# Layer-0 attention by half-groups, with the scores turned on TensorE

## What is computed

```python
# layer 0: 16 heads of 8 features
tp = silu(cond) @ Wt + bt                       # shift, scale and gate, twice, per sequence
h = layernorm(x, g1, be1) * (1 + scale_msa) + shift_msa
q, k, v = split(h @ Wqkv + bqkv)                # [B, 32, 16, 8] each
attn = softmax(einsum('blhd,bmhd->bhlm', q, k) * 8 ** -0.5)
h = einsum('bhlm,bmhd->blhd', attn, v) @ Wproj + bproj
x = x + gate_msa * h
h = layernorm(x, g2, be2) * (1 + scale_mlp) + shift_mlp
x = x + gate_mlp * (gelu(h @ W1 + b1) @ W2 + b2)
# layer 1: rmsnorm, FiLM, one head of 128 features, the same MLP without gates
```

## Time and profile before

| | |
|---|---|
| median of three runs | 284.4 us |
| profiled execution | 283.33 us, span 281.5 us |
| PE busy | 248.0 us (88% of the span) |
| DVE, ACT, POOL busy | 189.0, 164.7, 184.7 us |
| PE's clock, granted | 0.994 of full on average |
| chain that ended last | PE 55%, DVE 11%, DMA 10%, ACT 8%, issue 8% |
| DMA packets | 44569, of which 32512 under 512 B |

### The profile page before, as it was taken

One profiled execution on the slowest core, in us unless ns is written; L12 is line 12 of the kernel. 1 busy time (PEld: TensorE's weight loads), 2 busy tenths in 40 slices (PEclk: granted clock), 3 DMA queues, 4 the chain that ended last, 5 costly groups with the idle time before them and its releaser, 6 DMA issues.

```text
span 281.5 us, 8249 instructions
## 1 busy us (share of the span) xinstructions
PE 248.0 (88%) x2876; PEld 186.7 (66%) x2876; DVE 189.0 (67%) x535; ACT 164.7 (59%) x358; POOL 184.7 (66%) x187
## 2 busy tenths in 40 slices
PE   0677848689889898888999999999999989999996
...
GB/s 226 316 201 44 151 125 183 91 79 63 63 77 92 74 83 110 215 63 2 1 0 0 0 0 0 2 2 1 2 0 0 0 5 37 37 37 37 40 37 75
DMA packets 44569, 18.11 MB, mean 64 GB/s; under 512 B 32512, under 2 KB 43136, under 8 KB 44032
## 3 DMA queue, kind: packets, MB, share of 16 engines
...
q10 hardware_dynamic: 576, 1.98, 2.0%
...
## 4 chain that ended last, share of the span: by engine, by line
PE 55%; DVE 11%; DMA 10%; ACT 8%; issue 8%; SPq 3%; POOL 3%; ACTq 1%; DVEq 1%; POOLq 0%
PE bank L1086 20%; PE bank L948 17%; PE bank L978 5%; DMA values_scratch<-Vs 5%; PE bank L923 3%; DMA Vx<-values_scratch 3%; PE bank L991 2%; DVE hA L481 2%; ACT Kx L771 2%; DMA X<-x 2%; PE bank L1007 2%; ACT squares L886 2%; ACT xhat L756 2%; SPq L239 1%; PE bank L955 1%
## 5 line engine op out<-in xcount | busy, mean ns | idle before, releaser
L756 ACT ACTIVATE xhat<-X,shift,rstd 128x128 f32 (+1 forms) x96 | 39.4, 483 | 53.9 <-POOL shift L297 53.6
L1086 PE MATMUL bank<-W,Qx 128*128 128x128 f32 x512 | 59.6, 275 | 0.0
L1086 PEld LDWEIGHTS bank<-W,Qx 128*128 128x128 f32 x512 | 58.5, 192 | 1.0 <-issue 1.0
L948 PE MATMUL bank<-h,W 128*128 128x512 f32 x128 | 58.3, 595 | 0.0
L308 POOL TENSOR_TENSOR h<-hA,B 128x512 f32<-128x512 f32 x32 | 34.0, 1064 | 23.9 <-DVE hA L481 23.7
L806 ACT ACTIVATE Qx<-bank,col 128x512 f32<-128x512 f32 x64 | 39.1, 678 | 8.6 <-PE bank L948 8.6
L481 DVE TENSOR_TENSOR hA<-bank,A 128x512 f32<-128x512 f32 x32 | 22.0, 688 | 32.4 <-PE bank L923 16.6
L978 PE MATMUL bank<-Kx,Qx 128*128 128x128 f32 x256 | 35.4, 282 | 5.5 <-DMA Qx<-Qs 1.9
L948 PEld LDWEIGHTS bank<-h,W 128*128 128x128 f32 x128 | 22.9, 190 | 22.7 <-issue 22.4
L978 PEld LDWEIGHTS bank<-Kx,Qx 128*128 128x128 f32 x256 | 31.1, 192 | 7.4 <-DMA Qx<-Qs 2.1
L339 POOL TENSOR_TENSOR X<-yG,xg 128x512 f32 (+1 forms) x16 | 20.4, 1274 | 18.6 <-DVE yG L490 18.6
...
## 6 DMA issues: line engine op xcount, KB each, us to landing
values_scratch<-Vs SPq DMA_DIRECT2D x8, 288.0 KB, 2.4
...
Qx<-Qs SPq DMA_DIRECT2D x28, 64.0 KB, 2.3
...
```

What stands on the lines that cost most here:

```text
L756: last = act.activation(xhat[:, p, P * t:P * (t + 1)], X[:, x_tile(gg, t), :], ACT.Identity, bias=shift[:, p, t:t + 1], scale=rstd[:, p, t ...
L948: last = pe.matmul(bank[2 + n][:, :], w(f"W1_{phase // 2}", n), h[:, p, :], start=True, stop=True)
L1086: last = pe.matmul(y[t // 2][:, P * t:P * (t + 1)], gT[:, p, n, P * t:P * (t + 1)], w(f"W2_{phase // 2}", n), start=(n == 0), stop=(n == N ...
```

## The change

In layer-0 attention the unit becomes half a group: eight sequences, whose scores lie in two banks, the even sequences in bank 4 and the odd ones in bank 5.

- **Scores.** The keys, not the queries, are now spread over four masked copies, by four DMAs of 32 rows of 2 KB (`spread_k`); for groups 0 and 1 ACT and DVE make the copies (`place_k`). `Qx` is gone. Each sequence has four products of 32x32 weights with 128 columns, one for each quarter of PE's rows: 64 a group.
- **Turning.** The 32x32 transposes on DVE are replaced by 128x128 transposes on PE, eight for each half (`scores_T`), and the exponential reads them from PSUM.
- **Order.** PE's step is written anew and looped over groups 1 to 6; while it weighs the last quarter of a half it already waits for what the next scores need.
- **The last groups.** In group 6 the loop's queries and keys of "group 8" are the first two chunks of the MLP: their weights are loaded over Wq and Wk (`wup_in`), and ACT applies gelu to them there.
- **Values and gates.** The scratch buffer holds values by partition, so that a row is 2304 B in the store and 576 B in the loads. The first gate comes in eight pieces of a group each, one after each group's keys and values, the second in four pieces.
- **Update.** Bias, gate and residual are three passes: DVE adds the bias, POOL multiplies by the gate and POOL adds x. `keep` is gone from the first two phases.
- **Small ones.** -mean and var+eps in phase 0 are `tensor_reduce` instead of `tensor_scalar`. `bcol`, the memset of `Qx` and the masked query writes on DVE at the start are gone. The fold of the biases moves from the setup into group 0.

```diff
+        def of_half(half):
+            return range(half * GB // 2, (half + 1) * GB // 2)
+
+        def slot(b):
+            return b % (GB // 2) // 2
+
...
-            def spread_q(g, p):
-                wait(sp, s_ready, 4 * g - 4)
-                sp.wait_ge(qkv_moved, 2 * g + 1)
-                for a in range(HQ):
-                    sp.dma_start(Qx[L * a:L * (a + 1), p, :, a, :], by_seq(Qs[L * a:L * (a + 1), p, :])).then_inc(q_spread[p], 16)
...
+                sp.wait_ge(k_moved, g + 1)
+                sp.wait_ge(s_ready, 2 * g - 2)
+                for r in range(HQ):
+                    sp.dma_start(Kx[r:P:HQ, p, r, :], Ks[r:P:HQ, p, :]).then_inc(k_spread[p], 16)
+
+            def spread_v(g, p):
+
+                sp.wait_ge(v_moved, g + 1)
+                wait(sp, v_spread[p], 16 * HQ * (g // 2))
+                sp.dma_start(values_d[p], Vs[:, p, :]).then_inc(v_stored[p], 16)
+                sp.wait_ge(v_stored[p], 16 * (g // 2 + 1))
+                wait(sp, pv_done, 2 * g - 2)
+                src = values_d[p].rearrange("(q m) (r f) -> r m q f", q=TB, r=HQ)
+                for r in range(HQ):
+                    sp.dma_start(Vx[L * r:L * (r + 1), p, r, :].rearrange("m (q f) -> m q f", q=TB),
+                                 src[r]).then_inc(v_spread[p], 16)
+
+            def spread_gates(i, n, pieces):
+
+                size = NT // pieces
+                tiles = slice(n * size, (n + 1) * size)
+                wait(sp, gates_in[i], 16 * TB * n)
+                for b in range(TB):
+                    sp.dma_start(gate[L * b:L * (b + 1), i, tiles, :].rearrange("p t d -> p (t d)"),
+                                 gates_d[b:b + 1, i, tiles, :].rearrange("o t d -> o (t d)")
+                                 .broadcast_to([L, size * D])).then_inc(gates_in[i], 16)
...
+            spread_gates(0, 0, NG)
+            for g in range(1, NG):
+                spread_v(g, g % 2)
+                if g < NG - 1:
+                    spread_k(g + 1, (g + 1) % 2)
+                if g == NG - 2:
+                    sp.wait_ge(k_ready, NG)
+                    sp.wait_ge(q_ready, NG)
+                    at, up0 = W_AT["Wqkv"][0], W_AT["W1_0"][0]
+                    sp.dma_start(W[:, at:at + 2 * D], weights[:, up0:up0 + 2 * D]).then_inc(wup_in, 16)
+                spread_gates(0, g, NG)
+            sp.wait_ge(pv_done, 2 * NG - 1)
+            for n in range(NG // 2):
+                spread_gates(1, n, NG // 2)
...
                 at = x_group(g) if isinstance(g, int) else bass.ds((gg + NG) % NG * TG, TG)
-                pool.tensor_tensor(X[:, at, :], by_tile(yG[:, :]), by_tile(xg[:, p, :]), ALU.add).then_inc(x_updated, 1)
-
-            pool.memset(Qx[:, :, :, :, :], 0.0).then_inc(zeros_ready, 1)
+                pool.tensor_tensor(by_tile(yG[:, :]), by_tile(yG[:, :]), gate[:, phase, at, :], ALU.mult).then_inc(xg_ready, 1)
+                pool.wait_ge(xg_ready, gg + 1)
+                pool.tensor_tensor(X[:, at, :], X[:, at, :], by_tile(yG[:, :]), ALU.add).then_inc(x_updated, 1)
...
-                    dve.tensor_scalar(mk[:, p, :], mv[:, :, 0], -1.0, None, ALU.mult).then_inc(dve_chain, 1)
-                    dve.tensor_scalar(v_sb[:, p, :], mv[:, :, 1], 1e-5, None, ALU.add).then_inc(v_ready, 1)
+                    dve.tensor_reduce(mk[:, p, :], mv[:, :, 0:1], AX_X, ALU.add, negate=True).then_inc(dve_chain, 1)
+                    dve.tensor_reduce(v_sb[:, p, :], mv[:, :, 1:3], AX_X, ALU.add).then_inc(v_ready, 1)
...
+            def shift_scores(g, half):
+                row_max(g, half, 0)
+                subtract_max(g, half)
+                row_max(g, half, 1)
+
+            def place_k(g):
+                dve.wait_ge(k_moved, g + 1)
+                for r in (0, 1):
+                    last = dve.tensor_scalar(Kx[:, g, r, :], Ks[:, g, :], r_mask[:, r:r + 1], None, ALU.mult)
+                last.then_inc(k_placed, 1)
...
+            def exps(g, half):
+
+                hh = 2 * g + half
+                for odd in range(2):
+                    act.wait_ge(st_ready[odd], hh + 1)
+                    if odd == 0:
+                        wait(act, pv_done, hh)
+                    act.activation(PT[:, odd, :], bank[1 + 6 * odd][:, :], ACT.Exp).then_inc(pt_ready[odd], 1)
...
+                if not last:
+                    apply(g + 3, 1 - p, (2, 3))
                 if known(g, 0, NG - 2):
-                    move_q(g + 2, p, k if p == 0 else k + 1)
-
-            attention0(0, 0, 0)
-            with act.Fori(0, 2) as i:
-                attention0(i * 2 + 1, 1, i)
-                attention0(i * 2 + 2, 0, i + 1)
-            for g in range(5, NG):
-                attention0(g, g % 2, g // 2)
+                    move_k(g + 2, p)
+                    move_q(g + 2, p)
+                elif not last:
+                    act.wait_ge(q_ready, NG + 1)
+                    gelus(0, 0, (0,))
+                    act.wait_ge(k_ready, NG + 1)
+                    gelus(0, 0, (1,))
+
...
+            def wait_scores(g, p, half, k):
+
+                hh = 2 * g + half
+                wait(pe, s_shifted[0], hh)
+                wait(pe, s_copied, hh)
+                if half == 0:
+                    pe.wait_ge(q_moved, g + 1)
+                    if isinstance(g, int) and g < 2:
+                        pe.wait_ge(k_placed, 2 * (g + 1))
+                    else:
+                        pe.wait_ge(k_spread[p], 16 * HQ * k)
+
+            def scores0(p, half):
+
+                for b in of_half(half):
+                    for a in range(HQ):
+                        rows_of, at = slice(L * a, L * (a + 1)), rows_at(b, a)
+                        last = pe.matmul(bank[4 + b % 2][at:at + L, P * slot(b):P * (slot(b) + 1)],
+                                         Qs[rows_of, p, L * b:L * (b + 1)], Kx[rows_of, p, :, L * b:L * (b + 1)],
+                                         start=True, stop=True)
+                last.then_inc(s_ready, 1)
+
+            def scores_T(g, half):
+
+                hh = 2 * g + half
+                for odd in range(2):
+                    pe.wait_ge(s_shifted[odd], hh + 1)
+                    wait(pe, pt_ready[odd], hh)
+                    for n in range(GB // 4):
+                        at = slice(P * n, P * (n + 1))
+                        last = pe.transpose(bank[1 + 6 * odd][:, at], Ss[:, half, odd, at], ident[:, :])
+                    last.then_inc(st_ready[odd], 1)
+
+            def weigh0(g, p, half, following=None):
+
+                hh = 2 * g + half
+                for odd in range(2):
+                    pe.wait_ge(pt_ready[odd], hh + 1)
+                wait(pe, o_used, hh)
+                for a in range(HQ):
+                    if a == HQ - 1 and following is not None:
+                        wait_scores(*following)
+                    for b in of_half(half):
+                        at = L * (b % TB)
+                        to = b // TB % 2 * OW + a * HQ * VW
+                        from_ = P * slot(b) + rows_at(b, a)
+                        last = pe.matmul(bank[6][at:at + L, to:to + HQ * VW], PT[:, b % 2, from_:from_ + L],
+                                         Vx[:, p, :, at_v(b, a):at_v(b, a) + VW], start=True, stop=True)
...
+                scores0(p, 1)
+                scores_T(g, 0)
+                if first:
+                    rows_T(2, 0)
+                    film1()
+                else:
+                    output_T(g - 1, 1 - p)
+                if not last:
+                    values0(g + 1, 1 - p)
                 else:
                     pe.wait_ge(wmlp_in, 16)
-                    pe.wait_ge(qkv_moved, 2 * NG)
-                    up(1, 0, 0, (0, 1))
+                if first:
+                    fold(0)
                 pe.wait_ge(v_spread[p], 16 * HQ * (k + 1))
-                weigh0(g, p, 0)
-                scores0(g, p, 3)
-                if known(g, 0, NG - 1):
-                    values0(g + 1, 1 - p)
-                if not first:
-                    output_T(g - 1, 1 - p)
-                weigh0(g, p, 1)
-                if known(g, 0, NG - 1):
-                    pe.wait_ge(q_spread[1 - p], 16 * HQ * (k + 1))
-                    pe.wait_ge(kx_ready, HQ * (g + 2))
-                    scores0(g + 1, 1 - p, 0)
-                if not known(g, 0, NG - 1):
+                weigh0(g, p, 0, None if last else (g + 1, 1 - p, 0, k + p))
+                if not last:
+                    scores0(1 - p, 0)
+                if last:
+                    project0(g - 1, 1 - p)
+                scores_T(g, 1)
+                if first:
+                    fold(1)
+                    pe.wait_ge(ab_ready, 3)
+                elif not last:
+                    project0(g - 1, 1 - p)
+                if known(g, 0, NG - 2):
+                    keys0(g + 2, p)
+                    queries0(g + 2, p)
+                if last:
+                    pe.wait_ge(s_shifted[0], 2 * NG)
```

(18 more changed lines are left out.)

567 lines of the change are left out of this document (248 added, 319 removed).

## The result

The changed kernel takes 275.49 us (median of four runs, 274.80 to 276.22) against 285.25 for the kernel before, run beside it: ratio 0.965, 95% interval 0.959 to 0.971. The profiled executions are 276.22 us (span 274.4) and 283.33 us, 7.1 us apart. The predicted 280.7 us, on the scale of those two, misses by 4.5 us.

What follows compares the result with a forecast made beforehand. PE was taken to bound layer-0 attention at 11.8 us a group; setup, groups and passage summed to 2.6 us less, 280.7 us on the profiled scale, 281.8 us on the median's, range 277.5 to 288.5 us.

Steps and rivals of the forecast that it cites:

- the term for the scores: Layer-0 attention, each group: 64 small score products take PE 3.8 us, between 3.5 and 4.04.
- PE's work in a new group: Layer-0 attention: 6.17 us kept work, 3.8 scores and 1.85 transposes make 11.8 us a group, from 11.5 to 12.35.
- no cost of changing form: Low end for a group's scores: 3.5 us if PE loses nothing changing into and out of small tiles.
- Rival 2: Layer-0 groups: PE cheaper in small scores, transposes and changes of form, 11.3 us a group; 277 to 280 us, chance 0.23.
- The weighing: Layer-0 attention, each group: two runs of 32 products take PE 1.40 us.
- the round trips: Layer-0 groups: other engines and transfers return before PE needs them; first half's exponentials hidden by only 0.4 us.
- rival 3: Layer-0 half-groups: ACT's exponentials come late and PE waits; 0.5 us per half gives 288.8 us, chance 0.17.
- Rival 4: Layer-0 groups: keys late behind SP's queue, PE waits 1.5 us; 291 us in six groups, 284 in one or two; chance 0.07.
- rival 5: PE's clock falls from setup waits or many transposes: 283.5 us if once, 293 if in each group; chance 0.07.
- The setup: Before the attention loop: first scores at about 19.5 us, loop's first step at 23.0 instead of 25.93.
- The end: Group 7 takes 11.15 us with two table loads of 1.28 us; passage into the MLP 7.55 instead of 7.08.
- small gate pieces: Layer-0 gate traffic in 256 KB pieces behind transfers PE needs: stalls of groups 1 and 2 go, together 6.1 us gained.

Runs made afterwards that it cites:

- Experiment 1: Changed kernel with odd sequences' score products on the same PE quarters as the even ones, four tiles instead of eight: 285.58 us against 276.22.
- experiment 3: Changed kernel plus six runs of 64 small products at its end, on one to sixteen tiles: 3.63 us for four tiles, 1.95 for eight.
- experiment 5: Changed kernel with PE's layer-0 attention loop removed, groups 1 to 6 written out: 280.70 us against 276.22.
- experiment 4: Changed kernel with PE's loop cut to two turns and groups 5 and 6 written out behind it: 277.31 us against 276.22.
- experiment 8: Changed kernel with ACT's exponential and gelu tables loaded ahead of use by one-column activations: median 272.88 us, ratio 0.963 to the kernel before.
- experiment 10: Side by side: changed kernel 274.60 us; with ACT's tables loaded early 272.68; with early tables and mean and variance by `tensor_scalar` 273.81.
- experiment 6: Changed kernel with layer 0's gates loaded in two large pieces behind groups 0 and 1: 279.79 us against 276.22.
- experiment 9: Changed kernel with negated mean and variance by `tensor_scalar` instead of `tensor_reduce`: 273.65 us against 276.22.
- experiment 7: Kernel before with only layer 0's gates loaded in eight one-group pieces: median 283.58 us against 284.37, ratio 0.997.

## Why the prediction was wrong

**The step that failed is the term for the scores in "PE's work in a new group"**: 3.8 us, with ends of 3.5 and 4.04, measured 2.16. The mechanism was right, that small products on different quarters share time, and the size was not. I took 0.055 us a product, a quarter of the 0.22 us of the earlier trace rows, because the earlier trace rows, a row with four tiles in turn, bore it out, and read `rows_at` without counting the tiles in it: the new code has eight. Experiment 1 gives the forecast's 1.88 us with four, experiment 3 gives 57 ns a product with four and 30 with eight. In the eight groups it is 13 us of PE's work too much, and experiment 1, with that work put back, takes 9.4 us more than the changed kernel; most of the rest is hidden in the setup and in groups 0 and 1, behind waits that are there either way. The lower end rested on "no cost of changing form", which leaves out that more may overlap; the bound from below should have been what is certain to be serial, one product at a time in each tile. Rival 2 had the right direction and too small a size (0.5 us a group, by small things), which is why the range ended at 277.5.

**The weighing** was put at 1.40 us by the two runs of the earlier trace rows and took 1.80. The loop has half of the 0.4: where the same group is written out (experiment 5) the two runs take 0.86 and 0.75 us. In group 7, whose first weighing has no waits for the next scores in it, it takes 0.69 (105.88 to 106.57). What makes the other 0.2 no run here tells.

**PE is the bound, and the round trips are hidden: right.** 10.34 of 10.39 us busy, over 97%, clock 1.00, no DMA wait in the middle groups. The first half's exponentials, which I held the tightest place (rival 3), show nowhere but in group 7. Rival 4 appeared once each in four variants, small: 0.26 us in experiment 4, 0.46 in experiment 5, 0.3 in experiment 8 and 0.82 in experiment 10. The clock stayed at 1.00 through middle groups with 24 transposes each. By the rule of the Trainium skill that rival 5 weighs ("TensorE: Matmul & The Clock Gate", Part 4) more was to be feared than came. Where the clock did fall in the attention of layer 0, PE had stood still before: 1.88 us in group 7 of the first profile, 1.85 and 1.84 there in experiments 1 and 3, 1.67 and 3.42 in group 1 of experiment 6, 1.67 in experiment 10. But 1.85 us in group 7 of experiments 9 and 10, and 1.95 us in group 1 of the first profile, were followed by no fall, and near the end of experiment 3 it fell with no standstill of more than 0.27 us ahead. The length of a standstill alone doesn't decide it, and no run here tells what does. The rule of the Trainium skill on one bank ("TensorEngine Tiling (Array Packing)", Gotcha 1) fails here again: in experiment 3 four row quarters into one bank take 3.63 us for 64 products, the same as into two.

**Missed: the reading of code.** I counted PE's loop over six groups at nothing. It is worth some 6 us against the same groups written out (experiment 5), and its first pass costs stalls in group 1, 1.5 to 3.1 us in the executions with small gate pieces. The kernel before showed no such stall there; it waited for values instead.

**The setup** was 1.4 us quicker: the first scores started 0.6 us earlier (18.93 instead of 19.5) and took 0.8 less. **The end**: group 7 was forecast at 11.15 with both table loads and takes 10.51 where the clock holds, 12.21 where it falls. The loads were where I put them, and 1.8 us could be had back (experiment 10).

**The small gate pieces** I took for the cure of groups 1 and 2. Alone they are worth nothing (experiment 7); without them the one execution of experiment 6 loses 3.6 us, and 5.7 against the changed kernel's fastest, in a longer stall and at a lower clock, not by late values. That the values are in time comes with the queries' transfer being gone; it was not tried apart.

The misses partly cancelled: 8.0 us less in the setup, group 0 and groups 2 to 6, 3.5 us more in groups 1 and 7. With the forecast's scores the kernel takes 285.6 us (experiment 1), and 280.7 was forecast on that scale: for its own premise the forecast was 4.9 us too low. A small slip stands in the group's sum: its high end adds up to 12.31 and not 12.35, and nothing hangs on it.
